# Relative attention: packed keys read in three wide transfers, packed queries read in two lanes

## The reference, cut to what matters

```
qh = (q @ Wq.T + bq)  -> 16 heads of 16         # q = layernorm(x), k = v = ctx
kh = (k @ Wk.T + bk);  vh = (v @ Wv.T + bv)
qk = einsum('bhqd,bhkd->bhqk', qh, kh)
r_k = table_k[clip(key - query, -128, 128) + 128]
attn = softmax((qk + einsum('bhqd,qkd->bhqk', qh, r_k)) / 4)
w1 = einsum('bhqk,bhkd->bhqd', attn, vh)
w2 = einsum('bhqk,qkd->bhqd', attn, r_v)        # r_v: the same rule from table_v
x  = x + tanh(g) * ((w1 + w2) @ Wo.T + bo)
```

## Time and profile before

| | us |
|---|---|
| median of 3 runs | 2842.71 |
| lowest, highest run | 2833.98, 2847.86 |
| the profiled execution | 2833.87 |
| its span, first to last instruction | 2832.1 |
| PE busy | 2023.6 (71% of the span) |
| DVE busy | 1274.1 (45%) |
| ACT busy | 836.0 (30%) |
| POOL busy | 559.0 (20%) |

### The profile page before, as it was taken

How to read it: one execution, slowest core, us unless ns; L and a number is a source line. 1 busy time by engine, 2 the same in 40 slices (tenths; PEclk the granted TensorE clock), 3 DMA queues, 4 the chain that set the end, 5 groups by cost and what they waited for, 6 DMA issues and landing times. The chain is left out here.

```text
span 2832.1 us, 62550 instructions
## 1 busy us (share of the span) xinstructions
PE 2023.6 (71%) x25380; PEld 1550.2 (55%) x25380; DVE 1274.1 (45%) x2419; ACT 836.0 (30%) x1484; POOL 559.0 (20%) x523
## 2 busy tenths in 40 slices
PE   4777777773775497978787878787847776766674
PEld 3455445542664376757576767575635554544452
DVE  3444444445774264645454545454516662111112
ACT  2333333321221132424242424242304551111110
POOL 1111111110000010101010101010010005888871
PEclk8889888876887577978787979787867677899985
DMA  4445454431223312222222222222011214656556
GB/s 97 83 87 94 91 97 87 87 70 58 67 67 114 64 43 46 65 43 64 45 61 47 62 46 65 43 62 46 16 43 49 74 58 118 126 116 131 129 114 189
DMA packets 255382, 216.84 MB, mean 77 GB/s; under 512 B 70101, under 2 KB 234431, under 8 KB 255025
## 3 DMA queue, kind: packets, MB, share of 16 engines
q1 hardware_dynamic: 221008, 178.48, 27.2%
q0 software_dynamic: 24576, 27.05, 5.7%
q10 hardware_dynamic: 9568, 7.87, 0.9%
HBM read 147.08 MB, written 72.45 MB: 78 GB/s over the span
## 5 line engine op out<-in xcount | busy, mean ns | idle before, releaser
L1397 PE MATMUL r_ps_s<-r_q,r_rk 96*128 96x32 bf16 x4096 | 266.2, 237 | 87.0 <-DMA r_q<-parts_scratch 72.5
L1397 PEld LDWEIGHTS r_ps_s<-r_q,r_rk 96*128 96x128 bf16 x4096 | 248.7, 123 | 112.4 <-issue 99.7
L1165 DVE TENSOR_TENSOR r_score<-r_score,r_ps_t 128x1024 f32<-128x1024 f32 x128 | 154.7, 1217 | 166.3 <-PE r_ps_t L1408 166.3
L1186 DVE TENSOR_TENSOR r_score<-r_ps_s,r_score 128x512 f32<-128x512 f32 x256 | 162.7, 684 | 128.2 <-PE r_ps_s L1428 127.3
L1273 ACT ACTIVATE r_score<-r_ps_s 128x512 f32<-128x512 f32 x256 | 152.9, 597 | 225.3 <-PE r_ps_s L1397 223.2
L1474 PE MATMUL r_ps_b<-r_score,r_rv 128*32 128x32 f32 x8192 | 180.7, 261 | 9.2 <-issue 9.1
L1428 PE MATMUL r_ps_s<-r_q,r_k 96*128 96x128 bf16 x1024 | 103.0, 239 | 104.0 <-DMA r_k<-parts_scratch 76.9
L1952 DVE TENSOR_TENSOR e_hT<-e_sil,e_ps_gu 128x256 f32<-128x256 f32 x64 | 27.0, 421 | 324.0 <-ACT e_sil L1974 324.0
L1474 PEld LDWEIGHTS r_ps_b<-r_score,r_rv 128*32 128x32 f32 x8192 | 154.2, 134 | 33.4 <-issue 33.1
L313 DVE TENSOR_REDUCE a_row_max<-a_ps_s 128x2 f32<-128x512 f32 (+1 forms) x192 | 127.4, 685 | 61.3 <-PE a_ps_s L478 55.3
L1913 POOL DMA_INDIRECT e_rows<-rows_w_scratch,k_token x128 | 134.9, 1054 | 98.9 <-DVE e_h_last L1940 60.1
(11 more groups left out here) (296 smaller groups left out, 4227.6 us busy)
## 6 DMA issues: line engine op xcount, KB each, us to landing
a_q<-parts_scratch SPq DMA_DIRECT2D x96, 128.0 KB, 4.2
a_k<-parts_scratch SPq DMA_DIRECT2D x96, 128.0 KB, 4.3
r_q<-parts_scratch SPq DMA_DIRECT2D x48, 256.0 KB, 4.1
r_k<-parts_scratch SPq DMA_DIRECT2D x48, 256.0 KB, 4.2
e_wg<-in_L_ffn_expert_wg SPq DMA_DIRECT2D x64, 128.0 KB, 2.3
e_wu<-in_L_ffn_expert_wu SPq DMA_DIRECT2D x64, 128.0 KB, 3.0
e_wd<-in_L_ffn_expert_wd SPq DMA_DIRECT2D x64, 128.0 KB, 3.3
rows_w_scratch<-m_row SPq DMA_DIRECT2D x8, 640.0 KB, 3.2
```

The lines of the kernel that those rows point to most:

```text
L1165: dve.tensor_tensor(part, part, bcast(ps_t[m % 2][:], NT), ALU.add).then_inc(shifted, 1)
L1186: dve.tensor_tensor(part, ps_s[c % 2][:], part, ALU.add).then_inc(added, 1)
L1397: ins = pe.matmul(ps_s[c % 2][:].rearrange("p (h q) -> p q h", h=BH)[:, n, :], rk6[:, j:j + P], q6[:, :, q], start=True, stop=True)
```

## The change

It does three things, all in relative attention.

The sixths are put in another order, local to this function: `Q_PARTS` (0, 0, 0, 1, 1, 2) and `K_PARTS` (0, 1, 2, 0, 1, 0). The six pairs are the same as before. Key parts now stand as hi mid low, hi mid, hi, so that three runs of neighbouring parts cover `k6`: 48, 32 and 16 partitions.

The key parts are written to scratch in another layout (`keys_i`), with the head dimension outermost, so that one partition of `k6` is one contiguous row of 16 KB, and the rows of hi, mid and low follow each other (`key_rows`). For this each key part of each batch is written in two transfers of 64 KB in place of one of 128 KB: 9 writes per batch in place of 6. `k6` is then read by three transfers of 768, 512 and 256 KB. The first two are `FIRST_KEYS`, ahead of the `r_w` transfers; the third is `LAST_KEYS`, behind them. Each still waits for the one before.

The six query reads stay as they are in size, but count on two semaphores in turn. Read `n` waits for read `n` - 2, so two are in flight.

```diff
--- before.py
+++ after.py
@@ -813,6 +813,9 @@
     LEFT = S - 1 - CLIP
     TAB = rk_t.shape[1]
     NW = 3 * P + 1
+    Q_PARTS, K_PARTS = (0, 0, 0, 1, 1, 2), (0, 1, 2, 0, 1, 0)
+    KEY_READS = ((0, 3), (3, 2), (5, 1))
+    NR = len(KEY_READS)
     with ExitStack() as stack:
         sb = lambda name, shape, dt: stack.enter_context(nc.sbuf_tensor("r_" + name, shape, dt))
         pb = lambda name, shape, dt: stack.enter_context(nc.psum_tensor("r_" + name, shape, dt))
@@ -869,7 +872,8 @@
         var_ready, rstd_ready, xn_ready = sem("var_ready"), sem("rstd_ready"), sem("xn_ready")
         projected, inputs_copied, hi_ready, rest_ready = (sem(n) for n in ("projected", "inputs_copied", "hi_ready", "rest_ready"))
         mid_ready, low_ready = sem("mid_ready"), sem("low_ready")
-        v_ready, v_placed, packed_out, packed_q, packed_k = (sem(n) for n in ("v_ready", "v_placed", "packed_out", "packed_q", "packed_k"))
+        v_ready, v_placed, packed_out, packed_k = (sem(n) for n in ("v_ready", "v_placed", "packed_out", "packed_k"))
+        packed_q = [sem(f"packed_q{n}") for n in range(2)]
 
         placed, place_copied, scored, added = sem("placed"), sem("place_copied"), sem("scored"), sem("added")
         key_maxed, turned, maxed, max_turned, shift_ready = (sem(n) for n in ("key_maxed", "turned", "maxed", "max_turned", "shift_ready"))
@@ -910,6 +914,9 @@
         heads_of = lambda a: a.rearrange("d (s e h) t -> d s e (h t)", s=NS, e=ND)
 
         pack_i = pack.rearrange("(i s) n e t -> i (s n e t)", s=NS).rearrange("i (n s e t) -> i n s e t", n=6, s=NS, e=D)
+        keys_i = pack.rearrange("(i s) n e t -> i (s n e t)", s=NS).rearrange("i (n d s e h t) -> i n d s e h t", n=6, d=DH, s=NS,
+                                                                              e=ND, h=HE)
+        key_rows = keys_i.rearrange("i n d s e h t -> i (n d) (s e h t)")
 
         def run(eng, step):
 
@@ -948,24 +955,30 @@
 
                 for n, done in enumerate((hi_ready, mid_ready, low_ready)):
                     sp.wait_ge(done, START + i * 8 + s * 4 + 2 * k + 2)
-                    sp.dma_start(pack_i[i, 3 * k + n, s].rearrange("(e p) t -> p e t", p=P), (q_parts, k_parts)[k][n][:])\
-                        .then_inc(packed_out, 16)
+                    if k == 0:
+                        sp.dma_start(pack_i[i, n, s].rearrange("(e p) t -> p e t", p=P), q_parts[n][:]).then_inc(packed_out, 16)
+                    else:
+                        for e in range(ND):
+                            sp.dma_start(keys_i[i, 3 + n, :, s, e], k_parts[n][:, e, :]).then_inc(packed_out, 16)
 
             def take_queries(i, first=False):
 
-                sp.wait_ge(packed_out, START + i * 192 + 192)
+                sp.wait_ge(packed_out, START + i * 288 + 288)
                 if not first:
                     sp.wait_ge(scored, START + i * (2 * CH))
                 for n, part in enumerate(Q_PARTS):
-                    sp.wait_ge(packed_q, START + 96 * i + 16 * n)
-                    sp.dma_start(heads_of(q6[n * DH:(n + 1) * DH]), rows_of(pack_i[i, part])).then_inc(packed_q, 16)
+                    sp.wait_ge(packed_q[n % 2], START + 48 * i + 16 * (n // 2))
+                    sp.dma_start(heads_of(q6[n * DH:(n + 1) * DH]), rows_of(pack_i[i, part])).then_inc(packed_q[n % 2], 16)
 
             def take_keys(i, which):
-                for n in which:
-                    sp.wait_ge(packed_k, START + 96 * i + 16 * n)
-                    sp.dma_start(heads_of(k6[n * DH:(n + 1) * DH]), rows_of(pack_i[i, 3 + K_PARTS[n]])).then_inc(packed_k, 16)
-
-            FIRST_KEYS, LAST_KEYS = range(0, 3), range(3, len(K_PARTS))
+                for r in which:
+                    n, many = KEY_READS[r]
+                    sp.wait_ge(packed_k, START + 16 * NR * i + 16 * r)
+                    first = (3 + K_PARTS[n]) * DH
+                    sp.dma_start(k6[n * DH:(n + many) * DH].rearrange("p h t -> p (h t)"),
+                                 key_rows[i, first:first + many * DH]).then_inc(packed_k, 16)
+
+            FIRST_KEYS, LAST_KEYS = range(0, 2), range(2, NR)
 
             sp.dma_start(ctx_in[:], c_rows[0, 0]).then_inc(ctx_loaded, 16)
             sp.dma_start(x_in[:], x_rows[0, 0]).then_inc(x_loaded, 16)
@@ -1240,7 +1253,7 @@
                     n = k - QK
                     hi, bias = ((q_parts[0], bq), (k_parts[0], bk))[n // 2]
                     if n == 0:
-                        act.wait_ge(packed_out, START + i * 192 + s * 96)
+                        act.wait_ge(packed_out, START + i * 288 + s * 144)
                     act.activation(hi[:, n % 2, :], ps_proj[f % 2][:, 0:S], ACT.Identity,
                                    bias=bias[:, n % 2:n % 2 + 1]).then_inc(hi_ready, 1)
 
@@ -1386,7 +1399,8 @@
                     if front:
 
                         if c == 0 and t == 1:
-                            pe.wait_ge(packed_q, START + 96 * (i + 1) + 96)
+                            for n in range(2):
+                                pe.wait_ge(packed_q[n], START + 48 * (i + 1) + 48)
                         if c == 0:
                             pe.wait_ge(added, START + CH * (h + 1))
                         if c >= 2:
@@ -1419,7 +1433,7 @@
                     if front:
                         k, h0 = c // 8, 4 * (c % 8)
                         if c == 0 and t == 1:
-                            pe.wait_ge(packed_k, START + 96 * (i + 1) + 96)
+                            pe.wait_ge(packed_k, START + 16 * NR * (i + 1) + 16 * NR)
                         if c < 2:
                             pe.wait_ge(place_copied, START + CH * (h + 1) + 15 + c)
                         else:
```

## The result

| | median us | runs | ratio to before, 95% interval |
|---|---|---|---|
| before | 2840.5 | 2834.0 to 2847.9 | |
| changed | 2760.2 | 2750.4 to 2765.1 | 0.971 (0.967 to 0.975) |

The change gains 80 us. The forecast was 132 us, 2711 us, with a range up to 2742 us. The profiled execution of the changed kernel has a span of 2748.6 us, 83.5 us under the one of before. Lines of the changed file are 14 further down in this part: the q pass is L1411, the k pass L1442, the row pass L1477 and L1488.

The account below looks back on a forecast made before the run. It took PE's waits for query and key reads in rounds 1 to 7 as the bound: 45.7 + 69.8 + 15.7 (prologue) + 3 (clock) - 2 (late next) = 132 us, so 2711 us against the median 2842.7; range 2692 to 2742 us.

Parts of the forecast that it names:

- The two waits: PE's waits in rounds 1 to 7 for `k6`, 69.8 us, and `q6`, 45.7 us, would both go.
- extra writes: Six more key writes per round on SP would cost nothing; if their cover were gone, 15 us.
- The prologue: Before the rounds, queries would land 8.6 us earlier and keys save 7.1 us more, 15.7 us in all.
- Queries in two lanes: Six query reads, two in flight, would land 14 us after their start, before PE's row pass ends at 18.2.
- rival A: The second query lane brings nothing: reads still take 25.3 us, the 45.7 us wait stays, 2770 us; chance 0.08.
- Keys in three reads: The 768 KB key read would land in 7 us (bounds 4.2 and 12.6), the third at 33.9, before PE's 38.1.
- What is late next: Behind the waits, POOL's sum would be in time and DVE's last shift cost 0.3 us a round, -2 us in all.
- the clock's 3 us: In PE's q pass without the pause, two of eight product groups would run quick: 3 us gained over seven rounds.
- B: Rival: wide key reads are slow or PE finds other waits; 2727 to 2742 us; chance 0.13.
- C: Rival: slower, PE's clock stays at 0.50 in the k pass and row pass of `t` = 1; 2903 us; chance 0.02.

Follow-up runs that it names:

- e1_lanes_only: The kernel before with only the query reads changed, two in flight; key layout, writes and six narrow key reads as before: 2774.1 us, ratio 0.979.
- e2_wide_only: The changed kernel with its query reads issued one at a time again; key layout, writes and three wide key reads stay: 2772.6 us, ratio 0.977.
- e5_spread: `e1_lanes_only` with each sixth of `q6`, `k6` and the table on every sixth partition instead of 16 neighbours: 2717.4 us, ratio 0.958.
- e10_spread_lanes: `e5_spread` with two lanes for the key reads too, four reads ahead of `r_w` and two behind: 2700.1 us, ratio 0.952.
- e11_spread_only: The kernel before with only the partitions of the sixths changed, every sixth instead of 16 neighbours, reads one at a time: 2774.8 us, ratio 0.978.

## Why the prediction was wrong

*The two waits.* Right: 69.8 and 45.7 us gone, as forecast, and little else in their place (PE's wait for DVE ahead of its k pass is 23.1 us where it was 20.9, POOL's sum brings no new wait, and the last of the extra writes was issued by 1165.1, 4 us ahead of T0).

*The prologue.* 15.7 us forecast. The k pass started at 963.62 where it had started at 975.86, in a part that began 1.2 us later: 13.4 us.

*Queries in two lanes.* Landing of one read rose from 4.1 to 5.1 us; the six were out within 11.5 us and landed by about T0 + 16, forecast 14. The mechanism was right and rival A is out: `e1_lanes_only` has no query wait. The rule of the Trainium skill named for A ("DMA: Bandwidth & Descriptors", section "Rules for kernel authors") did not hold for these reads: six went out in 11.5 us instead of 21.3.

*Keys in three reads.* The 768 KB read took 10.0 us to land, 7 taken, inside the bounds of 4.2 and 12.6. It would have cost little: the keys were complete at about 1205.75 + 4.6 = 1210.4, ahead of the k pass at 1213.82.

*The step that failed* is "What is late next". It looked for engines that wait on a semaphore and found slack behind all of them. It counted the DMA engines' time only for whether two reads fit beside each other, and put what the reads cost anyone else on those engines at nothing, without a reason. PE's instructions come through them too, and PE paid 48.6 us for it. The page of before had the row all along:

```profile
PE 2023.6 (71%) x25380; PEld 1550.2 (55%) x25380; DVE 1274.1 (45%) x2419; ACT 836.0 (30%) x1484; POOL 559.0 (20%) x523
...
q8 instruction: 190, 3.11, 0.5%
```

190 transfers on a queue named "instruction", 3.11 MB, 16 KB each, beside 2 x 25380 products and weight loads of PE: one for every 267 instructions of PE. The Trainium skill tells of it in "Runtime: NRT & Kernel Launch", section "Instruction fetch mechanics": instructions are refilled in blocks of 16 KiB, 256 instructions, by DMA. The trace agrees, with one block for about that many. The section calls the cost of a new block mostly hidden; here it was not, as the stops show. The row pass runs 544 products with as many weight loads in 17 us, so a block each 4 us; the q pass has 288 in 20 us, a block each 9 us. The blocks of before came like that, 3.9 to 4.4 us apart in the row pass of the earlier trace rows and 9.1 us apart in its q pass. Below are the queues (packets, MB, share of 16 engines) in 6 us of the row pass, first of the kernel before (1201 to 1207 us), then of the changed one (1182 to 1188 us, the last 2 us of it inside PE's stop; the share passes 100%, as long packets that started here run on behind):

```profile
q1 hardware_dynamic: 134, 0.47, 35.3%
q8 instruction: 2, 0.03, 2.1%
```
```profile
q1 hardware_dynamic: 94, 0.91, 112.9%
```

Before, two instruction blocks came; in the changed kernel none did, and the reads filled the engines. The next block came while PE stood still. Below is that queue from 1188.7 to 1190.7 us; from 1180.3 to 1188.7 it has no row:

```profile
q8 instruction: 1, 0.02, 5.2%
```

That is one block (5.2% of 16 engines' 2 us are its 1.7 us). It began at 1188.79, 10.2 us behind the one before it, and had landed at 1190.44; PE went on at 1191.88, 1.4 us later. It is so in every long stop. The row passes of rounds 1 to 7 have 62 stops of over 1.5 us ("issue") in seven of the twelve kernels here, and none in the five others (before, `e2_wide_only`, `e5_spread`, `e10_spread_lanes`, `e11_spread_only`). In each of the 62 exactly one block lands, and PE goes on 1.2 to 2.0 us behind it. In the changed kernel's seven longest the block begins 2.8 to 4.1 us after PE has stopped.

There is also a stop with which to compare. Where the loop jumps back, before has five of 2.7 to 3.0 us:

```profile
1278.65 2.02 PE L1397 MATMUL r_ps_s<-r_q,r_rk 96*128 96x32 bf16 x32 [2.78 <-issue]
```

The block began at 1275.91, as soon as PE had stopped, and landed at 1277.08, 1.6 us before PE went on. All 60 such stops of the twelve kernels have one block, and PE goes on 1.5 to 1.8 us behind it. The long stops of the row pass end in the same way; what is longer is the time until the block begins.

So the sum lacked a term of 57.7 - 9.1 = 48.6 us, and 132 - 48.6 = 83.4 us; the spans differ by 83.5. That close a match is partly chance: the clock's 3 us did not come either (the granted clock went from 1.00 to 0.50 at 1190.3, 4.4 us into PE's stop, so the first four shift products of the q pass took 0.60 us at 1195.88), and the prologue gave 2 us less.

Shown by the runs: the stops grow with what the reads lay on the DMA engines while PE is in its row pass (one read in flight 5.8 us in all in rounds 1 to 7, two lanes 31.5, lanes and three key reads 53.7, six at once 65.5), they do not depend on the length of the runs or on the number of transfers, the stops of 6 us leave the row pass when the wide read does, they all but go when the same reads take less engine time, and each long one ends behind the landing of an instruction block. Not shown by an experiment of its own: no run changed the number of PE's instructions. Open: where a block waits before it begins, which the records do not say, and why the read into 48 partitions takes 8.6 to 10.4 us when the one into 32 takes 4.6 to 5.0.

*Rivals.* B had the right name for the outcome ("PE finds other waits") and the wrong ones, and ended at 2742. C did not come: the granted clock was 1.00 again from 1217.6 us on, 3.8 us into the k pass.

## What to carry to other kernels

A wait for a DMA that you remove by putting more in flight can be paid by whoever else lives on the DMA engines, and here that was PE with its 16 KB of instructions each 4 us: look for "issue" gaps inside straight code, and for the "instruction" queue. Put heavy reads beside stretches with few instructions per microsecond, and keep little in flight beside the dense ones. Before adding lanes, make each read cheaper: the same 256 KB went to partitions 6 apart in 3.3 us and to 16 neighbours in 4.1, and with that the two query lanes left 4.7 us of stops in place of 31.5.

## What the runs showed of the hardware

- PE stops inside straight code, without a wait in the program, when reads of 512 KB and more are in flight: 2.2 to 3.3 us under two reads of 256 KB, 5.8 to 7.1 us under 768 KB behind them, 4.6 to 9.4 us under six reads.
- PE's instructions come in transfers of 16 KB on a queue of their own, here one each 4 us in the row pass. A block takes 0.9 to 2.5 us once it has begun, and PE goes on 1.2 to 2.0 us after it has landed: 62 long stops, and 60 at a jump back.
- Which partitions a read goes to changes its time, with the same bytes and runs: 4.1 us to neighbours against 3.3 us to every sixth, 6.7 against 4.3 us of engine time for six.
- A row of 16 KB and four runs of 4 KB cost about the same: 768 KB landed in 10.0 and 10.4 us.
